# Distance attention: floors first, minima's small work on VectorE, values' products moved, exponentials in pairs

## The reference

```python
q2 = jnp.sum(q * q, axis=-1)
k2 = jnp.sum(k * k, axis=-1)
qk = jnp.einsum('bhid,bhjd->bhij', q, k)
d2 = jnp.maximum(q2[..., :, None] + k2[..., None, :] - 2.0 * qk, 1e-12)
attn = jax.nn.softmax(-jnp.sqrt(d2), axis=-1)
out = jnp.einsum('bhij,bhjd->bhid', attn, v)
out = out.transpose(0, 2, 1, 3).reshape(B, N, D)
return out @ wo.T + bo
```

## Time and profile before

| what | value |
|---|---|
| median of three runs | 3808.49 us |
| profiled execution, its own time | 3799.39 us |
| its span | 3797.3 us |
| TensorE's granted clock, mean | 0.907 of full speed |
| busy over the span: PE / DVE / ACT / POOL | 84% / 80% / 60% / 48% |
| distance stage, first scores to the end | 3098.7 to 3797.3 us |

### The profile page before, as it was taken

How to read it: one execution, slowest core, us unless ns; L and a number is a source line. 1 busy time by engine, 2 the same in 40 slices (tenths; PEclk the granted TensorE clock), 3 DMA queues, 4 the chain that set the end, 5 groups by cost and what they waited for, 6 DMA issues and landing times. The chain is left out here.

```text
span 3797.3 us, 55242 instructions
## 1 busy us (share of the span) xinstructions
PE 3184.6 (84%) x16225; PEld 1672.8 (44%) x16225; DVE 3031.4 (80%) x4845; ACT 2297.1 (60%) x2738; POOL 1814.5 (48%) x904
## 2 busy tenths in 40 slices
PE   7767888888997997877889999899987777877776
PEld 3322333332335886655523334499975531111111
DVE  6878999999995776865678988577757768888887
ACT  4776666667772334643446666522226549999998
POOL 0008998999993111011200000034436538999996
PEclk9878999999998998987879999999998877888888
DMA  4543333323322345955742334144444733344432
GB/s 127 200 175 121 144 146 145 145 96 145 124 69 74 110 152 162 207 139 187 248 136 73 77 72 95 48 101 89 88 78 159 204 105 105 115 127 120 129 117 84
DMA packets 313743, 478.18 MB, mean 126 GB/s; under 512 B 50839, under 2 KB 256280, under 8 KB 293134
## 3 DMA queue, kind: packets, MB, share of 16 engines
q1 hardware_dynamic: 256894, 408.82, 33.8%
q10 hardware_dynamic: 44432, 51.10, 5.0%
q0 software_dynamic: 12288, 16.79, 2.7%
HBM read 322.48 MB, written 153.91 MB: 125 GB/s over the span
## 5 line engine op out<-in xcount | busy, mean ns | idle before, releaser
L1225 PE MATMUL mamba_psum<-mamba_hc,scan_ident 128*128 128x512 f32 x1024 | 548.7, 643 | 90.1 <-DVE mamba_hc L1133 72.1
L3643 POOL TENSOR_TENSOR distance_dist<-distance_dist,distance_least_all 128x2048 f32<-128x2048 f32 x124 | 559.0, 4540 | 74.9 <-DMA distance_least_all<-distance_least_rows 74.8
L1156 DVE TENSOR_TENSOR_SCAN mamba_psum<-mamba_psum,mamba_drive 128x512 f32<-128x512 f32 x352 | 414.9, 1216 | 22.9 <-issue 10.5
L2784 DVE TENSOR_REDUCE causal_row_max<-causal_psum 128x1 f32<-128x512 f32 x512 | 333.0, 683 | 78.0 <-PE causal_psum L2854 68.0
L1225 PEld LDWEIGHTS mamba_psum<-mamba_hc,scan_ident 128*128 128x128 f32 x1024 | 175.8, 195 | 418.0 <-DVE mamba_hc L1133 254.9
L2743 ACT ACTIVATE causal_probs<-causal_psum 128x1024 f32<-128x1024 f32 x256 | 250.6, 1021 | 122.0 <-PE causal_psum L2877 121.8
L3819 PE MATMUL distance_psum<-distance_shared_k_stacks,distance_shared_q_stacks 102*128 102x512 bf16 x512 | 208.7, 504 | 116.9 <-DVE distance_least L3737 56.5
L3737 DVE TENSOR_REDUCE distance_least<-distance_psum 128x2 f32<-128x1024 f32 x256 | 294.2, 1213 | 8.3 <-PE distance_psum L3819 8.0
L3773 DVE TENSOR_SCALAR distance_dist<-distance_psum 128x1024 f32<-128x1024 f32 x192 | 227.0, 1219 | 80.5 <-PE distance_psum L3834 80.5
L1076 POOL TENSOR_TENSOR mamba_drive<-late_channels,scan_b_all 128x1024 f32<-128x1024 f32 x64 | 149.9, 2355 | 289.3 <-POOLq L32 289.3
L1120 ACT ACTIVATE mamba_psum<-mamba_dt,scan_a_neg 128x512 f32<-128x512 f32 x256 | 167.3, 683 | 140.8 <-DVE mamba_hc L1133 140.3
(11 more groups left out here) (473 smaller groups left out, 8593.3 us busy)
## 6 DMA issues: line engine op xcount, KB each, us to landing
distance_least_all<-distance_least_rows SPq DMA_DIRECT2D x32, 1024.0 KB, 4.7
scan_b_all<-bc SPq DMA_DIRECT2D x16, 1024.0 KB, 4.6
scan_c_all<-bc SPq DMA_DIRECT2D x16, 1024.0 KB, 6.6
mamba_b_all<-bc SPq DMA_DIRECT2D x16, 1024.0 KB, 5.1
mamba_c_all<-bc SPq DMA_DIRECT2D x16, 1024.0 KB, 7.1
choice_w<-L_ffn_w SPq DMA_DIRECT2D x16, 1024.0 KB, 5.4
z<-mamba_in_z SPq DMA_DIRECT2D x8, 1024.0 KB, 3.9
xc<-mamba_in_xc SPq DMA_DIRECT2D x8, 1024.0 KB, 3.9
```

Source lines behind the costliest of these rows:

```text
L1156: dve.tensor_tensor_scan(out, bank, drive[:, n % DRIVES], 0.0, ALU.mult, ALU.add).then_inc(h_ready, 1)
L1225: pe.matmul(ps[:, Y_BANK + m % 2], ident[:, :], hc[:, n % PRODUCTS], start=False, stop=(s == DS - 1)).then_inc(y_summed, 1)
L2784: dve.reduce_max(row_max[:, g % 2, u:u + 1], ps[:, u % 2], AX.X).then_inc(a_max, 1)
L3643: pool.tensor_tensor(dist[:, g % 2, kt], dist[:, g % 2, kt], least_all[:, g % 2], ALU.subtract).then_inc(shifted, 1)
```

## The change

On ScalarE both floors now come first. Then come the wait for the floored minima, their root (without a bias), and the roots of the quarters. The Relu of the minima and the copy of the turned minima have gone to VectorE: `clamp_least`, a tensor_scalar maximum in place on 128x16 in SBUF, is the last instruction of VectorE's step (after minima, `turn_back` and `add_bias(1)`), and `copy_least`, from PSUM to SBUF, follows the clamp of second unit 4. The exponentials are issued in pairs of quarters, 128x4096, except for the last group.

On TensorE the minima are turned after second unit 4 instead of 3. Of the values' products of `out`, kt 0 now follows first unit 7, where it stood between first units 6 and 7; kt 1 follows second unit 0 of the next step, where it stood after first unit 7. `project` parts 0 and 1 follow second units 5 and 6 instead of 4 and 5.

```diff
--- before.py
+++ after.py
@@ -3558,6 +3558,7 @@
         UNITS = GH * TT // 2
         ACT_UNITS = 2
         DVE_UNITS = UNITS - ACT_UNITS
+        LEAST_UNIT = 4
         BUFFERS = 3
         LAST = (NB - 1, NG - 1)
         K_LOADS = 2 * (len(STACK) + 1)
@@ -3690,13 +3691,9 @@
 
                         act.wait_ge(pv_done, n * TT + 1)
                         floor_scores(0)
-                        act.wait_ge(a_min, n * UNITS + UNITS + 1)
-                        act.activation(least[:, g % 2], least[:, g % 2], ACT.Relu, bias=minus_floor[:, 0:1]).then_inc(least_clamped, 1)
+                        floor_scores(1)
                         act.wait_ge(least_clamped, n + 1)
-                        act.activation(least[:, g % 2], least[:, g % 2], ACT.Sqrt, bias=floor[:, 0:1]).then_inc(least_ready, 1)
-                        floor_scores(1)
-                        act.wait_ge(least_turned, n + 3)
-                        act.copy(least_t[:, g % 2], ps[0:GH * TT, 7, 0:P]).then_inc(least_copied, 1)
+                        act.activation(least[:, g % 2], least[:, g % 2], ACT.Sqrt).then_inc(least_ready, 1)
                         for kt in range(TT):
                             if kt == 0:
                                 act.wait_ge(above_floor, (n + 1) * ACT_UNITS)
@@ -3706,14 +3703,17 @@
                                 act.activation(dist[:, g % 2, kt], dist[:, g % 2, kt], ACT.Sqrt).then_inc(sqrt_ready, 1)
                     if out is not None:
                         b, g = out
-                        for kt in range(TT):
-                            if is_last(out):
-                                act.wait_ge(last_shifted, kt + 1)
-                            else:
-                                act.wait_ge(shifted, (b * NG + g) * TT + kt + 1 + 2 * TT)
-                            act.activation(dist[:, g % 2, kt], dist[:, g % 2, kt], ACT.Exp, scale=-1.0).then_inc(p_ready, 1)
-                            if is_last(out) and kt == 0:
-                                load_gx(NB - 1)
+                        for kt in range(0, TT, 2):
+                            pieces = [slice(kt, kt + 1), slice(kt + 1, kt + 2)] if is_last(out) else [slice(kt, kt + 2)]
+                            for piece in pieces:
+                                if is_last(out):
+                                    act.wait_ge(last_shifted, piece.stop)
+                                else:
+                                    act.wait_ge(shifted, (b * NG + g) * TT + piece.stop + 2 * TT)
+                                act.activation(dist[:, g % 2, piece], dist[:, g % 2, piece], ACT.Exp,
+                                               scale=-1.0).then_inc(p_ready, piece.stop - piece.start)
+                                if is_last(out) and piece.stop == 1:
+                                    load_gx(NB - 1)
 
                 act.wait_ge(floor_set, 2)
                 run(act, step)
@@ -3736,6 +3736,14 @@
                             dve.wait_ge(least_turned, n + 1)
                         dve.tensor_reduce(least[:, g % 2, h * TT + 2 * j:h * TT + 2 * j + 2], ps[:, pair(UNITS + u)], op=ALU.min,
                                           axis=AX.X).then_inc(a_min, 1)
+
+                def clamp_least(b, g):
+                    dve.wait_ge(a_min, (b * NG + g) * UNITS + UNITS + 1)
+                    dve.tensor_scalar(least[:, g % 2], least[:, g % 2], D2_MIN, None, ALU.max).then_inc(least_clamped, 1)
+
+                def copy_least(b, g):
+                    dve.wait_ge(least_turned, b * NG + g + 3)
+                    dve.tensor_copy(least_t[:, g % 2], ps[0:GH * TT, 7, 0:P]).then_inc(least_copied, 1)
 
                 def shift_last():
                     b, g = LAST
@@ -3773,6 +3781,8 @@
                             dve.tensor_scalar(dist[:, g % 2, kt, j * 2 * T:(j + 1) * 2 * T],
                                               ps[:, pair(u)].rearrange("p h t -> p (h t)"), D2_MIN, None,
                                               ALU.max).then_inc(clamped, 1)
+                            if u == LEAST_UNIT:
+                                copy_least(*mid)
                     if proj is not None and not isinstance(proj, int):
                         add_bias(proj, 0)
                     if before is not None:
@@ -3793,8 +3803,11 @@
                     elif proj is not None:
                         finish_last(0)
                         finish_last(1)
+                    if first is not None:
+                        clamp_least(*first)
 
                 minima(0, 0)
+                clamp_least(0, 0)
                 dve.wait_ge(bo_loaded, DMA)
                 run(dve, step)
 
@@ -3874,19 +3887,19 @@
                     for u in range(UNITS):
                         if mid is not None:
                             second_scores(*mid, u)
-                            if u == 3:
+                            if u == LEAST_UNIT:
                                 turn_least(*mid)
-                        if before is not None and u in (2, 3):
-                            output(*before, u)
-                        if proj is not None and u in (4, 5):
-                            project(proj, u - 4, mid)
+                        if before is not None and u in (0, 2, 3):
+                            output(*before, max(u, 1))
+                        if proj is not None and u in (5, 6):
+                            project(proj, u - 5, mid)
                     for u in range(UNITS):
                         if first is not None:
                             first_scores(*first, u)
                         if proj is not None and u in (1, 2):
                             project(proj, u + 1, mid)
-                        if out is not None and u >= UNITS - 2:
-                            output(*out, u - UNITS + 2)
+                        if out is not None and u == UNITS - 1:
+                            output(*out, 0)
 
                 for u in range(UNITS):
                     first_scores(0, 0, u, False)
```

## The result

The changed kernel takes 3865.77 us (median of four runs, 3863.64 to 3874.98) against 3809.21 for the kernel before: a ratio of 1.0152, 95% interval 1.0134 to 1.017, so 57 us slower. Its profiled execution took 3864.81 us, with a span of 3863.1.

A forecast was written before the change was run, and what follows sets the result against it. Bound: a ring of TensorE and VectorE, its step set by how early TensorE's clock returns. +5.3 us a batch over 7.25 batches gave +38.5, 3838 profiled, plus 9.1 to the median: 3847 us, own range 3825 to 3862, overall 3797 to 3868.

The forecast's parts named there:

- rival C: POOL's subtractions hold VectorE's clamp of the minima; if not hidden, +1.3 us a step, 3866 us; chance 0.12.
- Step(w): Step length in us when TensorE's clock rises w us after M: 21.65 at 10, 22.15 at 11.
- price of the copy: VectorE's copy of the turned minima, between the clamps of second units 4 and 5: +0.25 us a step.
- The distance of the rise: TensorE's clock returns to 2.4 GHz 11.0 us after M, counting 4.1 us of unbroken run; range 10 to 12.
- M: The start of VectorE's first minimum of a group, from which times within a step are counted.
- The step behind a projection: Its clock, high throughout before, may now fall: 21.2 us, half way between 20.3 and 22.15.
- From the profiled execution to the median: 3838 us forecast for the profiled execution, plus 9.1 by which the old median stood above its profile: 3847.
- ScalarE's head: ScalarE from floor 0 to first root, 3.97 us before: net -0.45 to +0.9, cost 0 beside the ring.
- the ring: The chain of waits between TensorE and VectorE taken to set the step, with ScalarE next.
- Pairs: ScalarE's exponentials in pairs save 0 to 0.64 us a step, nearer 0.1 to 0.2, counted as 0.
- Rivals A and B: A: clock back before the last first-score product, 3800 us, chance 0.20. B: rise keeps its distance, 3804.5 us, chance 0.13.
- The order as such: TensorE's new order of products alone gains 0.3 us a step if the clock comes back where it did.

The follow-up runs named there:

- e4: The changed kernel with the clamp of the minima back on ScalarE; 3867.8 us, ratio 1.0161 to the kernel before.
- e11: e6 with the exponentials issued one by one instead of in pairs; ratio 0.9939 to the kernel before.
- e1: The changed kernel with only the values' products put back in their old places; 3821.0 us, ratio 1.0035 to the kernel before.
- e9: e8 with four more unread matmuls filling the break ahead of the last first-score product; ratio 1.0018 to the kernel before.
- e10: e9 with the clamp of the minima back on ScalarE; ratio 0.9989 to the kernel before.
- e2: The kernel before with only the values' products moved to their new places; 3845.9 us, ratio 1.0103 to the kernel before.
- e6: e5 with unread matmuls added behind first-score products to keep the clock high; 3776.6 us, ratio 0.9942 to the kernel before.
- e7: The kernel before with the same added unread matmuls as e6; 3788.3 us, ratio 0.9970 to the kernel before.
- e3: The changed kernel with three unread matmuls in the break ahead of the last first-score product; 3843.5 us, ratio 1.0092 to the kernel before.
- e8: The changed kernel with e6's added unread matmuls, the break ahead of the last first-score product left open; 3831.8 us, ratio 1.0089 to the kernel before.
- e5: e1 with the clamp of the minima back on ScalarE; 3813.4 us, ratio 1.0036 to the kernel before.

## Why the prediction was right

The forecast was 3847 us with a range from 3797 to 3868; it came to 3865.8. The direction and the mechanism were the forecast's, the size was short: +38.5 forecast, +57 measured. The time lies above the forecast's own range (3825 to 3862) and 2 us inside the overall one, whose upper end was there for rival C, and C costs this kernel nothing (e4). C's own number, 3866, is met by chance, and so it is luck that the overall range held.

- **The step as a function of the rise.** Step(w) = 0.47w + 16.95 gives 21.65 for the rise at 10.0 and 22.64 for 12.1; the trace has 21.84 and 22.71. This held, and so did its price of the copy (0.25; 0.27 measured). With the measured rises in all four steps, and the forecast's 1.28 for the projection, it gives 91.6 us a batch against 92.2 measured.
- **The distance of the rise.** Here the sum was mis-sized; w is the distance of the rise from M. I took w = 11.0 for every step, from an unbroken run of 4.1 us at the opening. Measured are 10.0, 12.1, 13.3 and 12.4, mean 12.0. The two plain steps cancel nearly (21.84 + 22.71 = 44.55 against 44.3), the projection's step is 24.74 against 23.4.
- **The step behind a projection.** I took half way between 20.3 and 22.15; the clock falls in it in every batch (PEclk 0.85 in the fourth row of the windows), and it takes 22.87 against 21.2. These two terms are 3.0 of the 3.3 us a batch that the forecast lacked: 92.2 against 88.9.
- **From the profiled execution to the median.** The sum gave 3838 for the profiled execution, which took 3864.8, so the steps were 27 us short. The 9.1 us by which the kernel before's median stood above its profile were added; in the changed kernel they are 1. This brought the forecast 8 us nearer, by luck.
- **ScalarE's head.** Forecast between 0.45 less and 0.9 more, beside the ring. Measured from floor 0 to the first root 4.73 us, against 3.97, with 1.84 us idle ahead of floor 0. That it costs nothing no run tests by itself.
- **Pairs.** 0 was right (e11, at the high clock).
- **Rival C.** Its mechanism is there, 0.17 to 4.05 us. I had it over by M+10.4; in the step shown it lasts to M+11.15, because POOL started at M+2.1 (3486.26) and not M+1.0. Behind a projection POOL started at M-0.3 (3531.34), the clamp missed the end of its second subtraction and was held to the end of the third, M+13.3. That it costs nothing in this kernel was right by luck of the clock: s2 is late as well, and e4, without the hold, takes as long. In the old order or at a high clock it costs (e1, e9 against e10).
- **Rivals A and B** (the clock back as early as now): behind the stage's opening no step of the changed kernel had its rise before M+10.0.
- **The order as such.** The forecast had the new order gain 0.3 us a step if the clock comes back as early as before. At w = 10.0 the whole change gains 0.1 (21.84 against 21.94). At the high clock the new order alone costs the kernel before 0.1 (e2) and the kernel with the floors in front 0.8 (e10 against e6, 0.47%; the clock over the stage is 0.92 and 0.94). The formula counts o0 behind f7 rightly, but was only held against the old kernel. There the turn of the minima waits for their root, and the clamp of s4 starts at M+14.3 however early s2 is (s2's clamp at M+10.4 before, at M+11.2 in e2). With the floors in front and the turn behind s4 this wait is gone, the clamp of s4 starts at M+13.4 in e6, and the step is 0.7 shorter (e6 against e7, 19.5 against 20.2); the new order gives that back, at M+14.2 in e10. I had worked out the sum of the two and not seen that the useful half needs no new order.

The Trainium skill's "SBUF — State Buffer", section "Who interferes with whom", says of a VectorE instruction in a two-port mode and a GpSimd one that the instruction that comes second is blocked fully until the first ends. The 4.56 us for 16 columns in e1, over just when POOL's subtraction is, agree with it.

Left open: how much of the gain of e6 over e7 is the turn's new place and how much the floors', which weren't tried apart; and what sets the moment of the rise. That the break delays it is shown by e3 and, for the falls, by e8 and e9, but e3 has no break from f6 on and still rises at 9.0 to 11.5, where the kernel before has 7.0 to 10.0.

## What to carry to other kernels

Look at the granted clock step by step before you judge an order of work on TensorE: here an order that leaves a break of 1.2 us in front of the matmuls that everyone waits for cost 1.0% (e2), 0.6% came back with the break filled (e3), and unread matmuls in breaks made the kernel before 0.3% faster, and 0.6% with the floors and the minima turned too. Put matmuls that don't wait into a wait that is there anyway: at the high clock o0 was free ahead of f7 and cost 0.8 us a step behind it (e6, e10). Once the clock is steady, the effect of each edit can be read; here, while it wasn't, an edit of 1.6 us in a step was paid back by the clock somewhere else (e5). Be wary of a small VectorE instruction between SBUF tensors beside long POOL instructions on a path that something waits for: 16 columns took up to 4.56 us here.

## What the runs showed that I had not expected

In the changed kernel, and in e2 to e5, a step's rise of the clock repeats to 0.1 us from batch to batch, and an edit in one step moves it by several us in others: e1 and e5 differ in the clamp alone, 1.6 us in one step of four, and the rises go from 9.2 to 10 us after M in most steps to 7.0 to 12.4. No single run length gives the rise. From the start of f7, with the break ahead of it, it took 3.1 to 6.4 us in the changed kernel; from the start of f6, without a break, 2.4 us at the least in the kernel before (step of 3515.56) and 6.8 at the most in e3. Counted from f3, with waits of some 0.1 us between the units, these two are 5.8 and 10.2. And a break of 1.66 us at the high clock ended with the clock down in the changed kernel behind a projection and at 1.00 in e2 at the same place.
